# First sweep of a graph-network kernel: where GpSimd waits for the landing of its row gathers

## What is computed

```python
x_l = (x @ W_l + b_l).reshape(n, H, F); x_r = (x @ W_r + b_r).reshape(n, H, F)
m = leaky_relu(x_l[src] + x_r[dst] + (ea @ W_e).reshape(-1, H, F), 0.2)
alpha = einsum('ehf,hf->eh', m, att)          # then a softmax over the edges of a target
out = segment_sum(x_l[src] * alpha[..., None], dst).mean(heads)   # batch norm, relu
```

## Time and profile before

| | |
|---|---|
| median of 3 runs | 6867.18 us (6836.62 to 6873.22) |
| profiled execution, span from first to last instruction | 6810.8 us |
| what the median has beyond that span | 56.4 us |
| busy: PE, DVE, ACT, POOL | 4219.0, 3344.2, 1439.7, 3619.4 us |
| gathers of the first sweep (POOL L585) | 256 + 1308, first at 81.49 us, last at 2830.8 us |

### The profile page before, as it was taken

One profiled execution on the slowest core, in us unless ns is written; L12 is line 12 of the kernel. 1 busy time (PEld: TensorE's weight loads), 2 busy tenths in 40 slices (PEclk: granted clock), 3 DMA queues, 4 the chain that ended last, 5 costly groups with the idle time before them and its releaser, 6 DMA issues. The chain is left out here.

```text
span 6810.8 us, 81310 instructions
## 1 busy us (share of the span) xinstructions
PE 4219.0 (62%) x16760; PEld 3105.7 (46%) x16761; DVE 3344.2 (49%) x8382; ACT 1439.7 (21%) x6145; POOL 3619.4 (53%) x3589
## 2 busy tenths in 40 slices
PE   4777777777777777768999998533333333333335
PEld 3555555555555555644444445333333333333335
DVE  6444444444444444479999998822222222222224
ACT  1111111111111111236666663400000000000000
POOL 2555555555555555305555551056666666666662
PEclk8888888888888888879999998755555555555555
DMA  6333333333333333324343441201111111111111
GB/s 106 92 93 95 93 93 94 95 99 95 96 93 93 98 92 93 98 81 124 110 111 109 110 112 50 57 20 23 23 23 23 23 23 23 23 23 23 23 23 28
DMA packets 609795, 478.35 MB, mean 70 GB/s; under 512 B 424696, under 2 KB 438034, under 8 KB 609334
## 3 DMA queue, kind: packets, MB, share of 16 engines
q1 hardware_dynamic: 440940, 256.05, 14.3%
q0 software_dynamic: 101184, 104.41, 7.2%
q10 hardware_dynamic: 67465, 115.81, 4.7%
HBM read 348.37 MB, written 126.73 MB: 70 GB/s over the span
## 5 line engine op out<-in xcount | busy, mean ns | idle before, releaser
L1417 POOL DMA_INDIRECT BR<-h2D,mS x1564 | 1476.9, 944 | 1007.4 <-issue 451.5
L585 POOL DMA_INDIRECT BR<-hD,AL x1308 | 1247.2, 953 | 1018.4 <-ACT ZR L634 638.4
L1441 PE MATMUL PS<-BR,ZR 128*128 x3328 | 796.1, 426 | 1507.1 <-DVE ZR L544 1086.3
L616 PE MATMUL PS<-Wz,BR 128*128 128x264 f32 x3328 | 1209.0, 449 | 696.3 <-DVE alq L682 319.0
L1441 PEld LDWEIGHTS PS<-BR,ZR 128*128 128x128 f32 x3328 | 735.9, 328 | 1567.3 <-issue 1563.9
L679 DVE SCALAR_TENSOR_TENSOR PS<-PS,a 128x528 f32<-128x528 f32 x832 | 594.8, 715 | 1543.4 <-PE PS L617 653.6
L1460 DVE TENSOR_TENSOR BR<-BR,PS 128x64 f32 x1664 | 362.6, 218 | 1725.3 <-remote 1306.5
L617 PE MATMUL PS<-BR 128*128 x3328 | 1150.8, 431 | 0.0
L940 PE MATMUL PS<-BR,ZR 128*128 128x329 f32 x3328 | 1027.9, 469 | 27.0 <-POOL BR L926 21.0
L616 PEld LDWEIGHTS PS<-Wz,BR 128*128 128x128 f32 x3328 | 653.9, 219 | 839.0 <-issue 587.1
L926 POOL TENSOR_TENSOR BR<-ZR,BR 128x768 f32<-128x768 f32 x416 | 616.1, 1481 | 416.6 <-ACT BR L912 414.7
(11 more groups left out here) (254 smaller groups left out, 2641.4 us busy)
## 6 DMA issues: line engine op xcount, KB each, us to landing
zD<-ZR ACTq DMA_DIRECT2D x416, 256.0 KB
ZR<-zD SPq DMA_DIRECT2D x416, 256.0 KB, 2.7
BR<-relD SPq DMA_DIRECT2D x105, 512.0 KB
ZR<-ea SPq DMA_DIRECT2D x1664, 32.0 KB
BR<-h2D,mS POOLq DMA_INDIRECT x1564
BR<-hD,AL POOLq DMA_INDIRECT x1308
AL<-hD SPq DMA_DIRECT2D x28, 224.0 KB, 2.6
BR<-hD,lmS POOLq DMA_INDIRECT x256
```

What stands on the lines that cost most here:

```text
L585: Q.indirect_dma_start(HT[:, (t % G) * F:(t % G) * F + F], None, hD, bass.IndirectOffsetOnAxis(at_src, 0)).then_inc(hs[q % 16], 16)
L616: P.matmul(m, zo1[:, p % 2, (j % 2) * 128:(j % 2) * 128 + 128], Wz, start=True, stop=False)
L1417: Q.indirect_dma_start(BIG[:, j * F:j * F + F], None, h2D, bass.IndirectOffsetOnAxis(mS[:, (j // 16) % 4, j % 16:j % 16 + 1], 0)).then_inc ...
L1441: ins = P.matmul(bank3(j // 4)[:, j % 4, :], oh[:, (j // 4) % 4, j % 4, :], rows, start=True, stop=True)
```

## The change

Behind every eighth gather, that is behind the last one of fours 1, 3, 5 and so on (and behind the last of all), GpSimd now waits until the two fours it has just issued have landed, and raises `landed` by one for each. The wait behind each four for the four two before it goes, and so do the two waits at the end. The number of waits and of raises stays at one for each four, and the gathers, their order, their destinations and the credits of `hf` stay as they are.

```diff
             Q.indirect_dma_start(HT[:, (t % G) * F:(t % G) * F + F], None, hD, bass.IndirectOffsetOnAxis(at_src, 0)
                                  ).then_inc(hs[q % 16], 16)
-            if t % 4 == 3 and q >= 2:
-                Q.wait_ge(hs[(q - 2) % 16], 64 * ((q - 2) // 16 + 1)).then_inc(landed, 1)
-        for q in (NG3 // 4 - 2, NG3 // 4 - 1):
-            Q.wait_ge(hs[q % 16], 64 * (q // 16 + 1)).then_inc(landed, 1)
+            if t % 8 == 7 or t == NG3 - 1:
+                for done in range(q - t % 8 // 4, q + 1):
+                    Q.wait_ge(hs[done % 16], 64 * (done // 16 + 1)).then_inc(landed, 1)
         close(hf)
```

## The result

The kernel after takes 6514.74 us, the median of four executions (6500.76 to 6519.28), against 6870.2 us for the kernel before (four executions; the 6867.18 us ahead of the prediction are the median of three of them). The ratio is 0.9489, 95% interval 0.9462 to 0.9515: 5.1% faster, where the forecast was 1.6% (6756 us) and its range ended at 6600. The sign was right, the size was too small by a factor of three.

A forecast was written before the change was run, and what follows sets the result against it. No engine full: in the first sweep GpSimd's credits and TensorE's late signals hold each other up. Sixteen-gather cycles fall from 27.86 to 26.7 us, 96 times, 111 us: 6867 - 111 = 6756 us, range 6600 to 7000.

The forecast's parts named there:

- The bound and the sign: First sweep: engines hold each other up, none full; 809.2 us of credit waits hide the landing waits; faster, chance 0.52.
- the closure: First sweep: while joined fours of gathers are in flight, TensorE's signals come late, coming through when the run has landed.
- Two readings of the trace: First sweep: 1.73 us a slot a third slower than 1.17; nearly all 153 even fours gapped 0.30-0.70 us show the closure.
- The gap before even fours: GpSimd's pause between the odd four's last gather and the next even four: 1.80 us in place of 0.30, range 1.1-2.0.
- b and c joined, then the landing: Cycle of fours a, b, c, d (a = 3, 7, ...): c joins b, 6.5 to 16.2 us; d starts at 18.7.
- The next a is 8.0 us behind d: Cycle's last step: from four d's start to the next four a, 8.0 us with ScalarE's table read, closing 26.7 us.
- The median lies 56.4 us above that span: Whole kernel: the measured median taken as 56.4 us above the profiled span, forecast at 6700 us.
- All shifts by one four: Rival: credit starvation moves before even fours, runs become (even, odd), cycle stays 27.86 us, time 6867 us; chance 0.24.
- Credits pile up, eight at once: Rival: two credits ready at the landing, eight gathers go out at once, cycle 29.43 us, +151 us, 7018 us; chance 0.24.
- Closure gone, GpSimd's pace, 6400: Rival: late TensorE signals almost wholly go, GpSimd paces the first sweep at 23.0 us a cycle, 467 us less; chance 0.12.
- If GpSimd were what the sweep waits for: Dearest slower case: landing waits before even fours aren't hidden by credit waits, the whole 293 us is paid, 7160 us.

The follow-up runs named there:

- one fill: Kernel before with its own waits, plus one small GpSimd memset, waited for, behind each odd four of the first sweep; 6673.43 us, ratio 0.975.
- e1: Kernel after with the same landing waits moved behind even fours in place of odd ones; 6778.98 us, ratio 0.9912 to the kernel before.
- e3: Kernel after, but GpSimd waits for the landing of its own four behind every four of the first sweep; 6708.93 us, ratio 0.9813.
- e17: Kernel after plus one waited fill (small memset) behind every third-sweep four and behind even first-sweep fours; fourth chip, 6380.46 us, ratio 1.1519.
- e15: Kernel before plus three waited fills (small GpSimd memsets) behind every four of the first sweep; fourth chip, 6038.67 us, ratio 1.0903.
- e7: Kernel after, but GpSimd waits behind every twelfth gather for the landing of its last three fours; 6698.67 us, ratio 0.9784.
- e10: Kernel after plus one waited fill (small GpSimd memset) behind every fourth gather of the third sweep; 6465.5 us, ratio 0.9448.

## Why the prediction came out as it did, by its steps

- **The bound and the sign: right.** GpSimd's landing waits were hidden by its waits for credits, and the closure was cut: remote waits 1259 to 833 us (at least 100 us less was forecast). How much of the gain that cut makes is another matter: one fill brought half of the gain with none of it.
- **Two readings of the trace were wrong, neither a term of the sum.** 1.73 us a slot is not a third slower than 1.17 but half again as slow; a third of the time is what is lost. And of the even fours with a gap of 0.30 to 0.70 us not nearly all have the closure: counting remote waits of over 2 us that end from 1 us behind the four's start to 2.3 us behind its end, 95 of the 125 with 0.30 us have one, and none of the 30 with 0.32 to 0.9 us.
- **The gap before even fours: too small.** I took 1.80 us from one row as a start without credit trouble. It wasn't one: ScalarE's copy that gives this credit starts at 1240.86 and the gather 0.51 us behind it, as in the rows whose wait the profile puts down to the credit (1529.37 and 1529.88). Measured 2.27 and 2.35 in the mean, 2.24 in the median. The Trainium skill's 2.0 us for a GpSimd DMA ("DMA: Bandwidth & Descriptors", Anatomy of one DMA) gave an estimate of 2.3 us, and the trace agrees with it, 2.24 us. That costs 0.5 us a cycle and works against the miss.
- **b and c joined, then the landing: right.** Four c joins b in 96 of 96 cycles. From the start of b to that of d I walked 18.7 - 6.5 = 12.2 us; measured 9.7 + 2.35 = 12.05.
- **"The next a is 8.0 us behind d": the step that failed.** It came from the earlier trace rows, where d had started on a credit given at that moment, so that the next group of copies and the table read still lay ahead. In the kernel after, d starts on a credit that ScalarE gave before the landing was through (copy of 1514.45, start 1520.14; the median is 7.0 us), so ScalarE is further on. The read's credit mostly comes while d's four gathers are made. Measured 4.7 + 1.00 = 5.7 us. The terms of the cycle are 26.7 + 0.5 - 0.15 - 2.3 = 24.75 us, measured 24.97, since a four takes 4.76 us in the mean. Over 96 cycles that is 96 x 1.73 = 166 us of the 190 us by which the span (6700 forecast, 6509.8 measured) was missed; some 10 us lie in the later sweeps, the rest at the sweep's ends.
- **"The median lies 56.4 us above that span": wrong.** I read it as time around the span. Every execution of the experiments lies 1.3 us above its own span (after: 6511.15 us with a span of 6509.8). The 56.4 us were the distance between a quick execution, the profiled one, and the median of others. The kernel after showed 4.9. That is the other 51 of the 241 us.
- **The rivals.** *All shifts by one four*: no in the kernel after, yes in e1, where the waits stand where this rival's mechanism leaves the read uncovered. *Credits pile up, eight at once*: two credits were in hand at 42 of 96 starts of b, c joined b in all 96, and a joined d in 56 of 95. But a run of eight was the rule before too (a and b), and the cycle wasn't the 29 us of this rival. *Closure gone, GpSimd's pace, 6400*: half true. The cycle is near GpSimd's own 2 x (9.7 + 2.3) = 24.0 us plus the 1.0 us before four a, though the closure stays; it mostly no longer holds back a credit that is wanted. But GpSimd isn't the bound as in e3: it never had more than two credits in hand, so the credits come at the same 24.97 us, and which side sets that pace isn't shown. I gave this case 0.12 with the argument that b and c join. They do, and it matters less than I took.
- **"If GpSimd were what the sweep waits for", 7160 us: not the case where the kernel after ran.** On the fourth chip it is the bound, and the 293 us that the prediction names for that case come out at some 400 by the estimate above. The Trainium skill's advice to wait late on a DMA's semaphore (same page, Rules for kernel authors) went the wrong way for the sign here (ratio 0.9489). On the fourth chip e17, which has these waits beside its fills, gave 1.1519; e15's 1.0903 is of fills alone and doesn't bear on it.
- **What stays open.** What holds TensorE's signals back, and why it doesn't occur in the set on the fourth chip. With 2.2 us behind every four it was gone but for 14 us (e3), with 0.30 us, and in the first sweep with 1.1 us, it was there; no run shows the mechanism. Also open is how long a pause behind every four has to be: 1.1 us was too short in the first sweep, 2.3 us enough, and what lies between ran only where there was nothing to remove. And how the gain divides between the read that is covered, the shorter closure and the runs kept in step.

## What to carry to other kernels

Where two engines hold each other by credits, ask of each long step on the credit's way (here a 3 us table read once in sixteen slots) in front of which transfer it falls; a wait that fixes the phase of the runs can be worth more than taking the step off the way (here 5.1% against 1.8%). Walk the cycle with the credits that are in hand at each start, and don't take a distance from a row that began without any. And before a pause is kept as an improvement, time it on several chips: the same kernel was 19% faster in the set on one of four, and there the pauses are a loss.

## What the runs showed of the hardware

- ScalarE and VectorE waited up to 10.0 us at a time in the first sweep (12.6 in e7) for signals of TensorE that came late while GpSimd made gathers 0.30 us apart, on three chips; on a fourth there was no such wait in two profiles of over 6000 us each. A gather (944 ns) and the sweep without gathers (1438 us) take the same there, and the kernel before takes 1282 us less (5538.7 against 6820.28).
- A gather of 128 rows took 0.945 us of GpSimd and the next began 0.30 us behind it, on all four chips.
- From the end of the last gather to the first behind its landing: 2.24 us in the median in the kernel after, 2.30 us in e10, 2.29 us on the fourth chip (e17). Of the 2.24 us, 1.48 pass until the wait is through and 0.75 until the next gather.
- Removing the gathers (e4) raised TensorE's granted clock from 0.90 (150 to 2530 us of the kernel after) to 0.99 (400 to 2000 us), with TensorE busy 77% and 92% of the time. That fits the reading of the earlier trace rows.
